# The state-scan output of a selective-scan and expert layer kept in bf16 instead of f32

## The chip, the cores and the metric

The kernel runs on the 8 cores of one Trainium2 chip, each with two of the 16 sequences of the batch and no exchange between them. The time is that of the device for the slowest core, in microseconds (us).

## The reference

What is computed, cut to the part that matters, is one layer: a normalised input goes through a selective scan (16 states per channel, 1024 channels, 2048 steps per sequence) and through a feed-forward part with a shared and eight routed experts, and the sum of both is added to the input.

```python
# selective scan (per sequence; D = 1024 channels, N = 16 states, G = 8 groups)
xp = xn @ in_proj_w.T + in_proj_b;  u, v = split(xp)
delta = softplus(u @ delta_proj_w.T);  A = -exp(a_log)
Bmat = (u @ b_proj_w.T + b_proj_b).reshape(B, L, G, N)
u_conv = silu(causal_conv(u, conv_w, conv_b))
dA = exp(delta[..., None] * A);  dBu = (delta * u_conv)[..., None] * Bexp
def step(h, xs):
    da, dbu = xs
    h = da * h + dbu
    y = einsum('bdn,dn->bd', h, c_param)
    return h, y
attn = y * silu(v)
# feed-forward: shared expert, plus top 2 of 8 routed experts on one hidden tensor
out = x + attn + swiglu(xn @ w_shared_in) @ w_shared_out \
        + sum_e wdense[:, e] * (swiglu(xn @ w1_shared) @ w2[e])
```

## The kernel before, in words

Each core treats its 2 x 2048 positions in 8 chunks of 512 (TC), four per sequence. A chunk has four stages, each a block with a barrier at its end: normalisation and transposition (L392 to L470), the projections (L472 to L555), the main stage (`emit_main`, from L632) and the output (L563 to L600). Weights run through a ring of 8 slots of 256 KB that SyncE (SP) fills from a bf16 copy in memory, 4 slots per transfer (`emit_pulls`, L322).

The main stage first does the short convolution for the 8 groups of 128 channels, on ScalarE and VectorE, while GpSimd forms du, the product of the convolution and delta (L834). Then it runs 128 steps j: group gg = j // 16, state n = j % 16. In a step

- TensorE (PE) broadcasts the row of B for this state, multiplied with c, to all channels, into pBCb (L949);
- ScalarE (ACT) computes dA = exp(A * delta) (L686);
- VectorE (DVE) multiplies du with pBCb into dBu (L819), in bf16, and then runs the recurrence over the 512 positions as one instruction, `tensor_tensor_scan`, from dA, dBu and the carried state into hsc (L824);
- GpSimd (POOL) copies the last column of hsc into the carried state stt_t (L849) and adds hsc to the group's sum ysc (L853; for n = 0 it copies, L851). After the sixteenth state it multiplies ysc with v_s, the gate, into acc (L858).

dA, dBu, hsc, ysc and pBCb each have two buffers. In the first chunk of each sequence the scan starts from 0.0 and not from the state, which is why its group shows in two forms (256 and 768 instructions).

The feed-forward work is placed between these steps by tables of numbers written by hand: T_GAPS for TensorE (gate and shared products L880 and L897, routed experts L932), A_EVS for ScalarE, P_INS for GpSimd (the products a_s * b_bf into smid and hid, L845), and V_INS for VectorE (the products hid * gate into hg, L786; the sum over experts into racc, L803 and L805; acc plus the shared result, L795). All engines run their instructions in the order in which they are written. VectorE waits for sp_y, GpSimd's counter of finished sums, of two steps before; GpSimd waits for sv_sc, the scan's counter; ScalarE waits for the scan that has read dA's buffer.

The lines that the change touches are L252, where hsc is allocated; L824, which writes it; and L849, L851 and L853, which read it.

Of the kernel before, what the change touches and what calls it, by code (L numbers as in the profile page):

```python
# [7 lines left out]
F32 = mybir.dt.float32  # L8
BF16 = mybir.dt.bfloat16
# [9 lines left out]
TC = 512  # L19
# [178 lines left out]
def build(dbg=False):  # L198
# [33 lines left out]
    with ExitStack() as ctx:  # L232
        en = ctx.enter_context

        def T(name, shape, dt):
            return en(nc.sbuf_tensor(name, shape, dt))

        env = {}
# [10 lines left out]
        b_sb = env["b_sb"] = T("b_sb", [32, 4, TC], BF16)  # L249
        dA = env["dA"] = T("dA", [128, 2, TC], F32)  # L250
        dBu = env["dBu"] = T("dBu", [128, 2, TC], BF16)
        hsc = env["hsc"] = T("hsc", [128, 2, TC], F32)  # L252
        stt_t = env["stt_t"] = T("state", [128, 128], F32)
        ccr = env["ccr"] = T("ccr", [128, 8, 3], BF16)
        ysc = env["ysc"] = T("ysc", [128, 2, TC], F32)
# [711 lines left out]
```

## Time and profile before

| what | us |
|---|---|
| median of 2 runs | 5287.13 (5264.27 to 5309.99) |
| the profiled execution, device time | 5258.23 |
| its span on the slowest core, from the first to the last instruction | 5256.7 |
| spans of all cores | 5234.7 to 5256.7 |
| busy: TensorE, VectorE, ScalarE, GpSimd | 2774.2, 3250.8, 1676.8, 1870.2 |

The profile is of the slowest core, core 5. Its times are read as follows: an engine's busy time is the sum over its instructions; a group of instructions is all those of one line, engine, operation and shape; idle time stands with the instruction in front of which it lies, and with what ended it. A duration is from the start of an instruction to its end, whatever it may wait for in between.

### The profile page before, as it was taken

Reading aid. Unit: us, or ns where it says so; the run is one execution under the profiler, and the core shown is the slowest. Engines: PE = TensorE matmul, PEld = TensorE weight load, DVE = VectorE, ACT = ScalarE, POOL = GpSimd, SP = SyncE. Lnnn points to the kernel's source line nnn. Section 1 sums busy time; section 2 is a strip of 40 time slices with the busy share of each in tenths; the row PEclk is TensorE's granted clock in tenths of the full one; section 3 lists DMA queues with packets and bytes.
Section 4 is the critical chain, followed back from the end, with each engine's and each line's share of the span. In section 5 each row is a group of like instructions: output and inputs, shape, how many; then the busy total and the mean of one; then the engine's idle time right before and its main releaser. Section 6 shows DMA issues by size and latency. Waiting matters only on the chain. (4 is left out here: it accounts for less than half of the span.)

```text
span 5256.7 us, 45388 instructions; the slowest of 8 cores (5234.7 to 5256.7 us)
## 1 busy us (share of the span) xinstructions
PE 2774.2 (53%) x10240; PEld 1030.3 (20%) x10240; DVE 3250.8 (62%) x4304; ACT 1676.8 (32%) x2403; POOL 1870.2 (36%) x2320
## 2 busy tenths in 40 slices
PE   0025763556625755357635566257563576355663
PEld 0012221212202222122212122022221222121221
DVE  0014788268863788447882688637884478826886
ACT  0014522353214712245213532147121452225321
POOL 0002544045430645126440454306441264403543
PEclk9997886678857988578866788568875788666885
DMA  9961121212211221112202122112211122121120
GB/s 104 110 94 66 66 83 42 82 40 75 83 35 64 74 74 67 42 64 72 85 34 82 42 74 86 46 50 74 74 67 40 59 74 82 42 80 43 67 90 19
DMA packets 51106, 348.50 MB, mean 66 GB/s; under 512 B 6368, under 2 KB 6624, under 8 KB 17024
## 3 DMA queue, kind: packets, MB, share of 16 engines
q1 hardware_dynamic: 46144, 302.30, 16.6%
q0 software_dynamic: 1632, 34.92, 6.2%
q10 hardware_dynamic: 3072, 8.39, 0.5%
q8 instruction: 95, 1.56, 0.1%
q14 instruction: 163, 1.34, 0.1%
HBM read 363.72 MB, written 51.38 MB: 79 GB/s over the span
## 5 line engine op out<-in xcount | busy, mean ns | idle before, releaser
L686 ACT ACTIVATE dA<-dlt,A_sb 128x512 f32<-128x512 bf16 x1024 | 740.1, 724 | 2009.5 <-DVE hsc L824 2007.4
L824 DVE TENSOR_TENSOR_SCAN hsc<-dA,state,dBu 128x512 f32<-128x512 f32 x768 | 1309.3, 1705 | 81.5 <-DVE dBu L819 1.8
L932 PE MATMUL pEG<-hg,ring 128*128 128x512 bf16 x4096 | 1013.6, 404 | 603.7 <-DVE hg L786 409.5
L853 POOL TENSOR_TENSOR ysc<-hsc,ysc 128x512 f32<-128x512 f32 x960 | 1234.0, 1285 | 2.0 <-issue 2.0
L819 DVE TENSOR_TENSOR dBu<-du,pBCb 128x512 bf16<-128x512 bf16 x1024 | 685.4, 669 | 458.4 <-PE pBCb L949 395.2
L849 POOL COPY state<-hsc 128x1 f32<-128x1 f32 x1024 | 242.3, 237 | 1661.4 <-DVE hsc L824 1645.1
L834 POOL TENSOR_TENSOR du<-du,dlt 128x512 bf16<-128x512 bf16 x64 | 73.6, 1150 | 1662.3 <-ACT du L673 1662.3
L932 PEld LDWEIGHTS pEG<-hg,ring 128*128 128x128 bf16 x4096 | 403.6, 103 | 1205.2 <-issue 831.9
L949 PE MATMUL pBCb<-b_sb,csel_sb 32*128 32x512 bf16 x1024 | 389.0, 422 | 418.6 <-DVE dBu L819 380.4
L824 DVE TENSOR_TENSOR_SCAN hsc<-dA,dBu 128x512 f32<-128x512 f32 x256 | 432.8, 1690 | 27.9 <-DVE dBu L819 1.8
L469 PE MATMUL pT<-ident,xnp 128*128 128x128 f32 x256 | 96.7, 446 | 583.6 <-DVE xnp L434 564.8
L880 PE MATMUL pAB<-xn_fm,ring 128*128 128x512 bf16 x1024 | 317.5, 466 | 78.7 <-ACT b_bf L700 78.6
L411 DVE TENSOR_SCALAR_CACHE_REDUCE uc<-x_tok 128x1024 f32<-128x1024 f32 x32 | 39.0, 1220 | 468.7 <-PEq L352 349.9
L590 PE MATMUL pT<-ident,accb 128*128 128x128 f32 x256 | 114.2, 446 | 306.6 <-DVE accb L574 306.6
L880 PE MATMUL pFF<-xn_fm,ring 128*128 128x512 bf16 x1024 | 249.7, 388 | 35.2 <-ACT b_bf L700 35.2
L728 DVE SCALAR_TENSOR_TENSOR uc<-u_pad,wcv_sb,uc 128x512 f32<-128x512 bf16 x192 | 165.1, 860 | 134.7 <-ACT uc L669 121.0
L949 PEld LDWEIGHTS pBCb<-b_sb,csel_sb 32*128 32x128 bf16 x1024 | 76.5, 94 | 747.6 <-issue 747.2
L720 DVE COPY u_pad<-ccr 128x24 bf16<-128x24 bf16 x6 | 1.1, 190 | 336.6 <-PEq L473 336.6
L786 DVE TENSOR_TENSOR hg<-hid,gb 128x512 bf16<-128x512 bf16 x512 | 207.9, 480 | 0.0
L579 DVE TENSOR_TENSOR x_tok<-x_tok,pT 128x128 f32<-128x128 f32 x256 | 73.8, 288 | 206.5 <-PE pT L590 206.5
L867 PE MATMUL pEG<-ident,lg 8*128 8x8 f32 x32 | 5.9, 220 | 352.5 <-DVE gt_tok L738 343.8
L686 ACT ACT_TABLE_LOAD x128 | 164.2, 1283 | 31.3 <-DVE hsc L824 28.3
(95 smaller groups left out, 2849.4 us busy)
## 6 DMA issues: line engine op xcount, KB each, us to landing
ring<-wsbf SPq DMA_DIRECT2D x256, 1024.0 KB, 4.8
wsbf<-wstream POOLq DMA_DIRECT2D x8, 4096.0 KB, 187.9
x_tok<-x SPq DMA_DIRECT2D x8, 2048.0 KB, 8.1
out<-x_tok SPq DMA_DIRECT2D x8, 2048.0 KB, 7.7
csel_sb<-cselbf ACTq DMA_DIRECT2D x64, 128.0 KB, 2.3
cselbf<-csel POOLq DMA_DIRECT2D x1, 1024.0 KB, 338.2
wbp_sb<-wbp POOLq DMA_DIRECT2D x1, 256.0 KB, 335.9
selc_sb<-selc SPq DMA_DIRECT2D x1, 128.0 KB
```

The source lines that it names most:

```text
L469: t.transpose(pT[:, j % 2, 0:128], xnp[:, j % 2, :], ident3[:]).then_inc(S.st_xp, 1)
L590: t.transpose(pT[:, j % 2, 0:128], accb[:, j % 2, :], ident3[:]).then_inc(S.st_op, 1)
L686: sc.activation(dA[:, j % 2, :], dlt[:, gg, :], AF.Exp, scale=A_sb[:, gg, n:n + 1]).then_inc(S.sa_da, 1)
L728: ins = v.scalar_tensor_tensor(uc[:, gg % 2, :], u_pad[:, gg, k:k + TC], wcv_sb[:, gg, k:k + 1], uc[:, gg % 2, :], ALU.mult, ALU.add)
L786: ins = v.tensor_tensor(hg[:, ii, kc, :], hid[:, kc, :], gb[:, e, :], ALU.mult)
L819: v.tensor_tensor(dBu[:, j % 2, :], du[:, gg, :], pBCb[:, j % 2, :], ALU.mult).then_inc(S.sv_bc, 1)
L824: v.tensor_tensor_scan(hsc[:, j % 2, :], dA[:, j % 2, :], dBu[:, j % 2, :], init, ALU.mult, ALU.add).then_inc(S.sv_sc, 1)
L849: gp.tensor_copy(stt_t[:, j:j + 1], hsc[:, j % 2, TC - 1:TC])
L853: ins = gp.tensor_tensor(ysc[:, gg % 2, :], hsc[:, j % 2, :], ysc[:, gg % 2, :], ALU.add)
L880: ins = t.matmul(pp[:, half, :], ring_piece(p_idx)[:, kc, :], xn_fm[:, kc, :], start=(kc == 0), stop=(kc == NK - 1))
L932: ins = t.matmul(pEG[:, m % 2, :], ring_piece(p_idx)[:, kc, :], hg[:, ii, kc, :], start=first, stop=(ii == 1 and kc == NK - 1))
L949: t.matmul(pBCb[:, j % 2, :], csel_sb[:, gg % 2, n, :], b_sb[:, s_, :], start=True, stop=True).then_inc(S.st_bc, 1)
```

## The change

The scan's output tile hsc is allocated in bf16 instead of f32. The scan instruction writes bf16, and GpSimd's three instructions that read hsc read bf16. The carried state, ysc, dA and dBu keep their types.

```diff
@@ -249,7 +249,7 @@
         b_sb = env["b_sb"] = T("b_sb", [32, 4, TC], BF16)
         dA = env["dA"] = T("dA", [128, 2, TC], F32)
         dBu = env["dBu"] = T("dBu", [128, 2, TC], BF16)
-        hsc = env["hsc"] = T("hsc", [128, 2, TC], F32)
+        hsc = env["hsc"] = T("hsc", [128, 2, TC], BF16)
         stt_t = env["stt_t"] = T("state", [128, 128], F32)
         ccr = env["ccr"] = T("ccr", [128, 8, 3], BF16)
         ysc = env["ysc"] = T("ysc", [128, 2, TC], F32)
```

No instruction changes its place. On GpSimd the copies out of hsc become conversions. This is GpSimd's order in the main stage at the end of a group of 16 states, before:

```order
L849 COPY state<-hsc 128x1
L853 TENSOR_TENSOR ysc<-hsc,ysc 128x512
L858 TENSOR_TENSOR acc<-ysc,v_s 128x512
L849 COPY state<-hsc 128x1
L851 COPY ysc<-hsc 128x512
```

And the same place in the changed kernel:

```order
L849 CAST state<-hsc 128x1
L853 TENSOR_TENSOR ysc<-hsc,ysc 128x512
L858 TENSOR_TENSOR acc<-ysc,v_s 128x512
L849 CAST state<-hsc 128x1
L851 CAST ysc<-hsc 128x512
```

The order is the same; L849 and L851 are CAST where they were COPY, and the additions of L853 have the same name with another type of input.

## Rows read from the trace of the kernel before

**Rows 1.** The page: span, and busy time of each engine.
```profile
span 5256.7 us, 45388 instructions; the slowest of 8 cores (5234.7 to 5256.7 us)
PE 2774.2 (53%) x10240; PEld 1030.3 (20%) x10240; DVE 3250.8 (62%) x4304; ACT 1676.8 (32%) x2403; POOL 1870.2 (36%) x2320
```

**Rows 2.** Busy time by stretch: the main stage of the second chunk, with its columns.
```profile
core 5: us, PE busy (x) PEld busy (x) DVE busy (x) ACT busy (x) POOL busy (x), PEclk, DMA share, GB/s
1103.00:1521.00 418.00, 265.42 (x970) 93.23 (x970) 343.99 (x355) 154.12 (x202) 221.77 (x279) 0.81 0.20 68
```

**Rows 3.** Groups by line: busy us, mean ns of one, idle before it and its releasers.
```profile
L824 DVE TENSOR_TENSOR_SCAN hsc<-dA,state,dBu 128x512 f32<-128x512 f32 x768 | 1309.3, 1705 | 81.5 <-DVE dBu L819 1.8
...
L819 DVE TENSOR_TENSOR dBu<-du,pBCb 128x512 bf16<-128x512 bf16 x1024 | 685.4, 669 | 458.4 <-PE pBCb L949 395.2 <-POOL ysc L853 45.8 <-POOL ysc L851 11.4
L824 DVE TENSOR_TENSOR_SCAN hsc<-dA,dBu 128x512 f32<-128x512 f32 x256 | 432.8, 1690 | 27.9 <-DVE dBu L819 1.8
```

**Rows 4.** Timeline of VectorE from 1254 us: start us, us, engine, line, instruction.
```profile
1254.04 1.28 DVE L824 TENSOR_TENSOR_SCAN hsc<-dA,state,dBu 128x512 f32<-128x512 f32 x1
1255.24 0.66 DVE L819 TENSOR_TENSOR dBu<-du,pBCb 128x512 bf16<-128x512 bf16 x1
1256.00 1.99 DVE L824 TENSOR_TENSOR_SCAN hsc<-dA,state,dBu 128x512 f32<-128x512 f32 x1
1257.92 0.66 DVE L803 COPY racc<-pEG 128x512 f32<-128x512 f32 x1
1258.50 0.67 DVE L819 TENSOR_TENSOR dBu<-du,pBCb 128x512 bf16<-128x512 bf16 x1
1259.28 1.40 DVE L824 TENSOR_TENSOR_SCAN hsc<-dA,state,dBu 128x512 f32<-128x512 f32 x1
```

**Rows 5.** Timeline of GpSimd beside it; in brackets its idle time before, and the releaser.
```profile
1255.51 0.18 POOL L849 COPY state<-hsc 128x1 f32<-128x1 f32 x1 [13.01 <-DVE hsc L824]
1255.65 1.26 POOL L853 TENSOR_TENSOR ysc<-hsc,ysc 128x512 f32<-128x512 f32 x1
1258.19 0.18 POOL L849 COPY state<-hsc 128x1 f32<-128x1 f32 x1 [1.28 <-DVE hsc L824]
1258.33 1.27 POOL L853 TENSOR_TENSOR ysc<-hsc,ysc 128x512 f32<-128x512 f32 x1
```

**Rows 6.** Timeline of GpSimd at the end of a group of 16 states.
```profile
1265.10 1.89 POOL L858 TENSOR_TENSOR acc<-ysc,v_s 128x512 f32<-128x512 f32 x1
1267.11 0.93 POOL L849 COPY state<-hsc 128x1 f32<-128x1 f32 x1
1267.98 0.61 POOL L851 COPY ysc<-hsc 128x512 f32<-128x512 f32 x1
```

**Rows 7.** Timeline of VectorE beside it, the two scans.
```profile
1264.63 1.40 DVE L824 TENSOR_TENSOR_SCAN hsc<-dA,state,dBu 128x512 f32<-128x512 f32 x1
...
1266.71 1.35 DVE L824 TENSOR_TENSOR_SCAN hsc<-dA,state,dBu 128x512 f32<-128x512 f32 x1
```

**Rows 8.** Single lines: ns min/median/max of one, first and last start us, forms.
```profile
L824 DVE TENSOR_TENSOR_SCAN hsc<-dA,dBu x256: 1224/1754/2311, 486.8 to 3351.5; 128x512 f32<-128x512 f32 x128
...
L853 POOL TENSOR_TENSOR ysc<-hsc,ysc x960: 1253/1264/2267, 490.4 to 5203.8; 128x512 f32<-128x512 f32 x192
...
L849 POOL COPY state<-hsc x1024: 174/183/1175, 488.3 to 5203.7; 128x1 f32<-128x1 f32 x171
...
L851 POOL COPY ysc<-hsc x64: 606/608/613, 488.4 to 5165.3; 128x512 f32<-128x512 f32 x64
...
L858 POOL TENSOR_TENSOR acc<-ysc,v_s x64: 1151/1890/2145, 538.4 to 5205.2; 128x512 f32<-128x512 f32 x64
...
L834 POOL TENSOR_TENSOR du<-du,dlt x64: 1145/1149/1153, 439.1 to 4769.4; 128x512 bf16<-128x512 bf16 x64
```

**Rows 9.** Who waited for L824's scan; what ended L819's idle time (us, times).
```profile
  POOL state L849: 1645.1, 811
...
  PE pBCb L949: 395.2, 198
```

## The prediction

> **What bounds the kernel now.** I read the engine totals first. VectorE (DVE) is the busiest engine with 62% of the span, and GpSimd (POOL) works 36% of it [rows 1]. No engine is near full, so the totals alone name no bound. The chain that ended last is of no use here: it goes back only through the output stage of the last chunk.
>
> Next, busy time by stretch. The main stage of the second chunk lasts 418 us, in which VectorE works 344 us and GpSimd 222 us [rows 2]. The change touches only instructions of this stage. Eight such stages are some 3.3 ms of 5.26 ms.
>
> Then the groups by line. The scans (L824) are the dearest: 1309.3 + 432.8 = 1742.1 us for 1024 of them, a mean of 1.70 us [rows 3]. Single scans differ widely, though all have one shape, and the timeline shows why. The scan at 1254.04 takes 1.28 us, and no GpSimd instruction runs beside it. The one at 1256.00 takes 1.99 us, and it starts while L853's add runs, which lasts from 1255.65 to 1256.91 [rows 4, 5]. The slow scan ends at 1257.99, 1.08 us behind the end of the add. The next one starts at 1259.28 and ends at 1260.68, again 1.08 us behind the end of an add (1258.33 + 1.27 = 1259.60). In the other direction L858 takes 1.89 us where its shortest takes 1.15 [rows 8]: it starts at 1265.10, the scan beside it ends at 1266.03, and it ends 0.96 us later, at 1266.99. The scan that started at 1266.71 ends 1.07 us behind that [rows 6, 7]. So a scan and a GpSimd instruction that reads SBUF don't run through together here: whoever came second ends as if it had begun to stream when the first was done.
>
> The Trainium skill, page "SBUF — State Buffer", section "Who interferes with whom", says the same: a VectorE instruction with two SBUF inputs contends with a GpSimd instruction that reads SBUF, and the loser blocks fully. By this rule the trace agrees (1.08 us behind the add, three times). Without it GpSimd would have slack and this change would be worth nothing.
>
> That gives the chain of one step. Scan j ends at 1255.32. GpSimd's 128x1 copy (L849) starts 0.19 us later, the add (L853) 0.14 us after that, takes 1.26 us, and scan j+1 ends 1.08 us behind it: 0.19 + 0.14 + 1.26 + 1.08 = 2.67 us, and scans do end at 1255.32, 1257.99 and 1260.68. By its semaphores VectorE waits little for GpSimd (45.8 + 11.4 us before L819 in the whole span) [rows 3], and it shows no idle time for this chain: the wait stands inside the scan's own duration. L853 is thus on the path, though its engine is idle for 1.27 us in each step.
>
> **The change part by part.** hsc, the scan's output, becomes bf16. Nothing is moved on any engine, and no wait is added or taken away. Four kinds of instruction touch hsc.
>
> 1. L853, 960 times, now reads bf16 (hsc) and f32 (ysc) and writes f32. Before, both inputs are f32 and it takes 1.253 us at least and 1.264 in the median. The trace has other two-input GpSimd instructions of the same 512 columns: L858 (f32 and bf16 in, f32 out) with 1.151 us at least, and L834 (all bf16) with 1.149 in the median [rows 8]. Both are multiplications while L853 is an addition, so the 0.11 us between them may belong to the type or to the operation; nothing in the trace tells these apart. The ends are 1.15 us (type) and 1.26 us (operation). Above them, should the addition convert its bf16 input in a pass of its own, at the rate of L851's copy (0.608 - 0.183 = 0.425 us for 511 columns), it would be 1.69 us. I take 1.151, the row with exactly the new mix of types: 1.264 - 1.151 = 0.113 us less.
>
> How often does this reach the end? 811 times GpSimd's L849 waited for the scan [rows 9], which are the steps in which the chain above starts afresh. 198 times VectorE sat idle before L819 until TensorE had delivered (395 us together) [rows 9]; there a scan that ends earlier only lengthens this idle time, if TensorE doesn't itself come earlier. I take all 198 off: 811 - 198 = 613 steps x 0.113 = 69 us. With all 811 it would be 92 us. In the steps with an expert accumulation (L803) between two scans, the scan is held up by only 1.40 - 1.28 = 0.12 us [rows 4], so the 0.113 still fits, but a second 0.1 us would find VectorE itself as the bound.
>
> 2. L849, 1024 times, becomes a conversion (CAST) of one column. From its start to that of the add it holds the chain for 0.14 us. L851's copy shows that columns cost 0.83 ns each, so the 0.18 us of L849 are fixed cost. It can't give back more than 0.14 us (613 x 0.14 = 86 us), and if its fixed cost doubled it would take as much. No GpSimd conversion stands in the trace. I take zero, the nearest row being the copy itself.
>
> 3. L851, 64 times, becomes a conversion of 512 columns: 0.61 us now. Between the fixed 0.18 us and a two-input instruction's 1.15 us this is -27 to +35 us. I take zero.
>
> 4. L824, 1024 times, writes bf16 and reads as before. Between L819, which writes bf16, and L803, which writes f32, there is nothing (0.66 us both) [rows 4], so I take zero. Its free duration is twice theirs for the same columns, which is the recurrence and not the write, so I exclude a gain. A loss as large as the spread between the shortest scan (1.224) [rows 8] and the usual free one (1.28) would be 0.06 x 1024 = 57 us.
>
> Sum: the profiled execution took 5258 us (span 5257). 5258 - 69 = 5189 us, 1.3% less. The median of the two runs of before is 5287, with the profiled time near the lower of them (5264); I predict for runs like the profiled one.
>
> **A rule that speaks against it.** L834, all bf16, takes 1.149 us; less the fixed 0.183 of L849 this is 0.966 us for 512 columns, or 1.89 ns each, where L853 has 2.11 ns. The Trainium skill, page "GPSIMD Engine Reference", section "2.1 Instruction dispatch", calls about 2.5 cycles per element a floor of every two-input body, whatever the types, since both operands come through one port; at its 1.2 GHz that is an estimate of 2.08 ns. By that rule L853 can't get faster, which is the outcome of the first rival below, 5258 us. L853 agrees with the rule; L834 and L858 are below its floor, so the trace shows that it isn't one for every type or every operation.
>
> **The rivals.**
> - The 0.11 us belong to addition against multiplication. Then L853 stays at 1.26 us and the time at 5258 us (up to 5287 by the median). For it: both fast rows are multiplications, and L858 with one bf16 input is no slower than L834 with two, so bytes as such don't count. Against: an addition and a multiplication would have to cost differently on the same data path, while two f32 operands are twice the bytes of two bf16. The same time comes out if the steps counted above hide the gain, by TensorE.
> - Slower: conversion costs GpSimd a pass of its own. With 1.69 us for L853 the chain grows by 0.425 us in 613 steps: +261 us, 5519 us. It decides over 2% from 105 / 613 = 0.17 us per step, and the one-column CAST could add to it. Against: L858 takes a bf16 input at 1.15 us. For: an in-place addition with a bf16 first input and the CAST stand nowhere in the trace.
> - More than forecast: the add falls to 1.15 in all 811 steps (-92 us) and the CAST gives a few hundredths too, 0.03 x 613 = 18 us: 5148 us, 2.1% less. For: shorter steps bring TensorE's inputs earlier too. Against: the expert steps have only 0.12 us to give.
> - The change does nothing to speeds, as the scan has no bf16 output path of its own and the type is dealt with elsewhere: the order of instructions shows L849 and L851 as CAST and the scan's output tile as bf16, so I give this nothing.
>
> **How the numbers follow.** Forecast (5189, own range 5166 to 5215): 0.58. No change (5240 to 5300): 0.26. More than forecast (5100 to 5165): 0.09. Slower by a pass or by the CAST (over 5300): 0.07. The range reaches from 5145 to 5300. The bound of 2% is 105 us, about what a measurement of this kernel can tell from no change; the forecast with its 69 us is inside it. Faster by over 2%: 0.09; within 2%: 0.84; slower by over 2%: 0.07.
>
> **What would show it right or wrong.** Right: L853's median is about 1.15, scans of the held-up kind go from 1.99 to 1.88 us and still end 1.08 us behind the add, the scans' sum falls from 1742 by some 80 us, the free scan stays at 1.28, and the main stage goes from 418 to about 409 us. Operation, not type: L853 stays at 1.26. Wrong from the start: L853 is faster, but scans stay at 1.99, which would mean that they aren't held by the add's end. If L849 starts the add later than 0.14 us behind it, the CAST is to blame. If all this is right and idle time before L819 grows by tens of us, TensorE took the gain.

## The result, and the profile after

The changed kernel takes 5174.0 us (median of 11 runs, 5167.3 to 5238.4), the kernel before 5268.7 us in the runs beside it. The ratio is 0.9813 with a 95% interval of 0.9785 to 0.9841: 1.9% faster. Medians and ranges here are of all executions; the ratios leave out those in which the cores of one die show a lower granted clock and take longer. The profiled execution took 5168.05 us, 90.2 us less than that of before.

Read the totals first. The page of the changed kernel, span and busy time of each engine:

```profile
span 5166.5 us, 45196 instructions; the slowest of 8 cores (5146.2 to 5166.5 us)
PE 2717.3 (53%) x10048; PEld 1022.9 (20%) x10240; DVE 3188.5 (62%) x4304; ACT 1671.4 (32%) x2403; POOL 1752.9 (34%) x2320
```

GpSimd lost 117 us of busy time and VectorE 62 us [rows 1], though no instruction of VectorE got less to do. (TensorE's count of matmuls is lower because some records are missing, so its busy time can't be compared.)

The groups by line of the changed kernel, which answer to [rows 3] (busy us, mean ns of one, idle before it and its releasers):

```profile
L824 DVE TENSOR_TENSOR_SCAN hsc<-dA,state,dBu 128x512 bf16<-128x512 f32 x768 | 1267.7, 1651 | 81.5 <-DVE dBu L819 1.8
L853 POOL TENSOR_TENSOR ysc<-hsc,ysc 128x512 f32<-128x512 bf16 x960 | 1128.3, 1175 | 2.0 <-issue 2.0
...
L819 DVE TENSOR_TENSOR dBu<-du,pBCb 128x512 bf16<-128x512 bf16 x1024 | 684.4, 668 | 430.0 <-PE pBCb L949 389.1 <-POOL ysc L853 31.2 <-POOL ysc L851 5.0
L824 DVE TENSOR_TENSOR_SCAN hsc<-dA,dBu 128x512 bf16<-128x512 f32 x256 | 418.4, 1634 | 27.9 <-DVE dBu L819 1.8
```

The scans fell from 1742.1 to 1686.1 us, which is 56.0 of VectorE's 62 us. The idle time before L819 fell by 28.4 us, from 458.4 to 430.0. Of these, 21.0 us are waits for GpSimd (45.8 + 11.4 before, 31.2 + 5.0 now) and 6.1 us are waits for TensorE (395.2 to 389.1). VectorE's shorter instructions and this shorter idle time are 62.3 + 28.4 = 90.7 us together, which is about the gain of the profiled execution, 90.2 us.

Single lines of the changed kernel, which answer to [rows 8] (ns min/median/max):

```profile
L824 DVE TENSOR_TENSOR_SCAN hsc<-dA,dBu x256: 1223/1884/2218, 486.2 to 3297.7; 128x512 bf16<-128x512 f32 x128
...
L853 POOL TENSOR_TENSOR ysc<-hsc,ysc x960: 1147/1158/2147, 489.7 to 5113.1; 128x512 f32<-128x512 bf16 x192
...
L849 POOL CAST state<-hsc x1024: 173/183/1192, 487.6 to 5113.0; 128x1 f32<-128x1 bf16 x171
...
L851 POOL CAST ysc<-hsc x64: 607/608/613, 487.7 to 5076.0; 128x512 f32<-128x512 bf16 x64
```

L853 went from 1.264 to 1.158 us. The two conversions cost what the copies cost: 183 and 608 ns in the median. The shortest scan, 1223 ns, is as short as before, so writing bf16 is worth nothing to the scan itself.

Timelines of VectorE and of GpSimd in the same place of the order as [rows 4] and [rows 5], in the changed kernel:

```profile
1237.09 1.28 DVE L824 TENSOR_TENSOR_SCAN hsc<-dA,state,dBu 128x512 bf16<-128x512 f32 x1
...
1239.05 1.89 DVE L824 TENSOR_TENSOR_SCAN hsc<-dA,state,dBu 128x512 bf16<-128x512 f32 x1
...
1242.22 1.29 DVE L824 TENSOR_TENSOR_SCAN hsc<-dA,state,dBu 128x512 bf16<-128x512 f32 x1
```

```profile
1238.56 0.18 POOL L849 CAST state<-hsc 128x1 f32<-128x1 bf16 x1 [13.44 <-DVE hsc L824]
1238.70 1.16 POOL L853 TENSOR_TENSOR ysc<-hsc,ysc 128x512 f32<-128x512 bf16 x1
1241.14 0.18 POOL L849 CAST state<-hsc 128x1 f32<-128x1 bf16 x1 [1.28 <-DVE hsc L824]
```

The add ends at 1239.86 and the scan at 1240.94, 1.08 us behind it, as before. The held-up scan went from 1.99 to 1.89 us with the add, and the one that follows L803 from 1.40 to 1.29. In the last one nothing is left: 1.28 us is a scan that nobody holds up.

### The profile page after: what moved, and what is told of

It reads as the page before. It is cut to its first block and busy times, and to the rows that moved or that the text cites. A ratio compares the mean times of both kernels' runs of the same rounds, so it can differ in the third digit from the quotient of the medians.

```text
span 5166.5 us, 45196 instructions; the slowest of 8 cores (5146.2 to 5166.5 us)
## 1 busy us (share of the span) xinstructions
PE 2717.3 (53%) x10048; PEld 1022.9 (20%) x10240; DVE 3188.5 (62%) x4304; ACT 1671.4 (32%) x2403; POOL 1752.9 (34%) x2320
## 5 line engine op out<-in xcount | busy, mean ns | idle before, releaser
L824 DVE TENSOR_TENSOR_SCAN hsc<-dA,state,dBu 128x512 bf16<-128x512 f32 x768 | 1267.7, 1651 | 81.5 <-DVE dBu L819 1.8
L932 PE MATMUL pEG<-hg,ring 128*128 128x512 bf16 x4000 | 999.7, 404 | 579.6 <-DVE hg L786 392.7
L853 POOL TENSOR_TENSOR ysc<-hsc,ysc 128x512 f32<-128x512 bf16 x960 | 1128.3, 1175 | 2.0 <-issue 2.0
L819 DVE TENSOR_TENSOR dBu<-du,pBCb 128x512 bf16<-128x512 bf16 x1024 | 684.4, 668 | 430.0 <-PE pBCb L949 389.1
L849 POOL CAST state<-hsc 128x1 f32<-128x1 bf16 x1024 | 227.8, 222 | 1687.3 <-DVE hsc L824 1673.4
L949 PE MATMUL pBCb<-b_sb,csel_sb 32*128 32x512 bf16 x1024 | 386.6, 420 | 404.7 <-DVE dBu L819 362.6
L824 DVE TENSOR_TENSOR_SCAN hsc<-dA,dBu 128x512 bf16<-128x512 f32 x256 | 418.4, 1634 | 27.9 <-DVE dBu L819 1.8
L880 PE MATMUL pAB<-xn_fm,ring 128*128 128x512 bf16 x992 | 298.7, 451 | 81.3 <-ACT b_bf L700 76.2
L786 DVE TENSOR_TENSOR hg<-hid,gb 128x512 bf16<-128x512 bf16 x512 | 204.5, 472 | 0.0
L469 PEld LDWEIGHTS pT<-ident,xnp 128*128 128x128 f32 x256 | 46.5, 182 | 633.3 <-issue 624.7
```

Of the source, the lines that this page charges most:

```text
L469: t.transpose(pT[:, j % 2, 0:128], xnp[:, j % 2, :], ident3[:]).then_inc(S.st_xp, 1)
L786: ins = v.tensor_tensor(hg[:, ii, kc, :], hid[:, kc, :], gb[:, e, :], ALU.mult)
L819: v.tensor_tensor(dBu[:, j % 2, :], du[:, gg, :], pBCb[:, j % 2, :], ALU.mult).then_inc(S.sv_bc, 1)
L824: v.tensor_tensor_scan(hsc[:, j % 2, :], dA[:, j % 2, :], dBu[:, j % 2, :], init, ALU.mult, ALU.add).then_inc(S.sv_sc, 1)
L849: gp.tensor_copy(stt_t[:, j:j + 1], hsc[:, j % 2, TC - 1:TC])
L853: ins = gp.tensor_tensor(ysc[:, gg % 2, :], hsc[:, j % 2, :], ysc[:, gg % 2, :], ALU.add)
```

## The experiments

Theory "lock": a scan that meets a GpSimd instruction which reads SBUF ends 1.08 us behind it, so that GpSimd's duration is on the path although its engine is idle for most of the time. Theory "type": L853 got shorter because one of its inputs is bf16. Rivals: additions differ from multiplications; the gain came with the scan's output or from GpSimd's load as such. All ratios are to the kernel before, run on the same chip.

**L853 as a multiplication, all in f32.** Kernel before, and the sum over states is left out:

```diff
-                                       ysc[:, gg % 2, :], ALU.add)
+                                       ysc[:, gg % 2, :], ALU.mult)
```

> Kernel before (hsc in f32), with L853 multiplying instead of adding; the sum over states is left out. Theory 'type' (two f32 inputs cost more than a pair with a bf16 one): L853 stays at 1.26 us and the time at that of before, about 5269 us, within 0.3%. Rival 'operation' (multiplications are faster on GpSimd than additions): L853 falls to 1.15 us and the time to about 5174 us, as the change gives.

Measured: 5261.7 us, ratio 1.0012 (0.9984 to 1.0040). L853 of this run:

```profile
L853 POOL TENSOR_TENSOR ysc<-hsc,ysc x960: 1252/1265/2258, 493.2 to 5221.3; 128x512 f32<-128x512 f32 x192
```

The median is 1265 ns against 1264 for the addition. "Operation" is out: the 0.11 us belong to the types. The time fell as expected too, within 0.3% of that of before.

**The sum in bf16 as well.** Changed kernel, with ysc in bf16:

```diff
-        ysc = env["ysc"] = T("ysc", [128, 2, TC], F32)
+        ysc = env["ysc"] = T("ysc", [128, 2, TC], BF16)
```

> Changed kernel, with the running sum ysc in bf16 too, so that L853 reads and writes bf16 alone. Theory 'floor' (one bf16 input already reaches what L834 has with two): L853 stays at 1.15 us and the time at that of the changed kernel, 5174 us, within 0.3%. Rival 'bytes' (each halved input takes 0.11 us off): L853 takes 1.05 us, and 811 steps x 0.11 = 89 us are gained again, 5085 us.

Measured: 5196.4 us in the median (5154.3 to 5227.2), ratio 0.9854 (0.9781 to 0.9928). The median is 0.4% above 5174, a little more than the 0.3% allowed, but the interval holds the changed kernel's 0.9813. L853:

```profile
L853 POOL TENSOR_TENSOR ysc<-hsc,ysc x960: 1139/1150/2149, 494.2 to 5164.4; 128x512 bf16<-128x512 bf16 x192
```

The second bf16 input, together with a bf16 output, is worth 8 ns (1158 to 1150) where the first was worth 106. "Bytes" is out, and "floor" holds for the duration. The time alone, with its interval of 0.7% to each side, would have told less than the line does; 5085 us would have been a ratio of about 0.965 and lies outside it.

**Only the sum in bf16.** The same line changed in the kernel before, so that hsc, the scan and L849 stay in f32.

> Kernel before with hsc left in f32 and only the running sum ysc in bf16. The scan, L849 and the input hsc are those of before. Theory 'lock and type' (the gain comes from L853's own duration alone, and it is any bf16 input that shortens it): L853 takes 1.15 us, held-up scans go from 1.99 to 1.88 us, and the time is that of the changed kernel, 5174 us, within 0.5%. Rival 'scan' (the gain comes with the scan's bf16 output, or with hsc as the first input): 5269 us, as before.

Measured: 5182.7 us, ratio 0.9851 (0.9807 to 0.9894), against 0.9813 (0.9785 to 0.9841) of the change itself. Groups by line:

```profile
L824 DVE TENSOR_TENSOR_SCAN hsc<-dA,state,dBu 128x512 f32<-128x512 f32 x768 | 1273.0, 1658 | 81.3 <-DVE dBu L819 1.8
L853 POOL TENSOR_TENSOR ysc<-hsc,ysc 128x512 bf16<-128x512 f32 x960 | 1122.0, 1169 | 2.0 <-issue 2.0
```

A scan that still writes f32 fell from 1309.3 to 1273.0 us in sum [rows 3], about as with the change (1267.7). So the scan's output type is not what shortened the scans; the add's duration is. (In this run the add's output is bf16 as well as its second input.)

**Half the add.** Changed kernel; the other 256 columns of the sum are left out:

```diff
-                ins = gp.tensor_tensor(ysc[:, gg % 2, :], hsc[:, j % 2, :],
-                                       ysc[:, gg % 2, :], ALU.add)
+                ins = gp.tensor_tensor(ysc[:, gg % 2, 0:256], hsc[:, j % 2, 0:256],
+                                       ysc[:, gg % 2, 0:256], ALU.add)
```

> Changed kernel, with L853 adding only the first 256 of 512 columns; the rest of the sum is left out. L853 should take 0.18 + 256 x 1.89 ns = 0.67 us, 0.49 us less. Theory 'lock': in a step without an expert accumulation a scan is held up until the add has ended, so the step goes from 2.57 to 2.08 us; in the 256 steps with one (L803, L805) the scan is hardly held up already and nothing is gained. (811 - 256) x 0.49 = 272 us, 4900 us, and up to 5000 us where TensorE or ScalarE becomes late. Rival 'GpSimd has slack' (its duration isn't on the path, the gain came otherwise): 5174 us, as the changed kernel.

Measured: 4985.8 us in the median of four (4910.1 to 5063.2), ratio 0.9336 (0.9291 to 0.9381). The two shortest executions, which the ratio is of, took 4910.1 and 4914.5 us, where 4900 had been expected. Single lines, of L824 and L853:

```profile
L824 DVE TENSOR_TENSOR_SCAN hsc<-dA,state,dBu x768: 1283/1319/2233, 1050.3 to 4859.0; 128x512 bf16<-128x512 f32 x192
...
L853 POOL TENSOR_TENSOR ysc<-hsc,ysc x960: 661/671/1586, 484.8 to 4860.7; 128x256 f32<-128x256 bf16 x192
```

The add takes 0.671 us, as worked out (0.67), and the median scan went from 1.88 to 1.32. VectorE's and TensorE's work is unchanged, and the kernel is 4.9% faster than the changed one (0.9336 / 0.9813). That is a gain of some 250 us from GpSimd alone, near the 272 expected; "GpSimd has slack" is out. A scan and the add that it meets, from the timelines of this run:

```profile
1188.42 1.40 DVE L824 TENSOR_TENSOR_SCAN hsc<-dA,state,dBu 128x512 bf16<-128x512 f32 x1
```

```profile
1188.07 0.67 POOL L853 TENSOR_TENSOR ysc<-hsc,ysc 128x256 f32<-128x256 bf16 x1
```

The add ends at 1188.74 and the scan at 1189.82, again 1.08 us later: the distance stays the same when the add is half as long.

**The scan reads one input from PSUM.** Kernel before. PSUM is the memory that TensorE writes its results to, and pBCb lies in it. L819 writes its product over pBCb, the scan takes it from there, and TensorE waits for the scan before it overwrites the buffer:

```diff
-            v.tensor_tensor(dBu[:, j % 2, :], du[:, gg, :],
+            v.tensor_tensor(pBCb[:, j % 2, :], du[:, gg, :],
                             pBCb[:, j % 2, :], ALU.mult).then_inc(S.sv_bc, 1)
...
-                                 dBu[:, j % 2, :], init,
+                                 pBCb[:, j % 2, :], init,
...
-                t.wait_ge(S.sv_bc, C_SVBC * c + j - 1)
+                t.wait_ge(S.sv_sc, C_SVSC * c + j - 1)
```

> Kernel before (hsc in f32), with L819 writing its product in place into pBCb in PSUM, and the scan reading it from there, so that the scan has only one input in SBUF. TensorE may overwrite a buffer of pBCb only after the scan, no longer after L819. Theory 'lock' (only a VectorE instruction with two SBUF inputs is held up): every scan takes about 1.28 us whatever GpSimd does, their sum falls from 1742 to about 1310 us, and up to 430 us are gained: 4840 us if nothing else is late, 5000 us where TensorE or ScalarE is. Rival 'no lock' (scans are held up in another way, as by the memory as such): scans stay at 1.99 us in the median and the time at 5269 us, or above it because TensorE waits longer.

Measured: 4852.3 us (4847.9 to 4858.8), ratio 0.9224 (0.9201 to 0.9247). (The 1.99 us in the expectation are the held-up scan of [rows 4]; the median of all scans before was 1.75 to 1.81.) All 1024 scans, and L849:

```profile
L824 DVE TENSOR_TENSOR_SCAN hsc<-dA,state,pBCb x768: 1279/1280/1283, 1056.4 to 4802.8; 128x512 f32<-128x512 f32 x192
L824 DVE TENSOR_TENSOR_SCAN hsc<-dA,pBCb x256: 1219/1221/1222, 490.6 to 3108.5; 128x512 f32<-128x512 f32 x128
...
L849 POOL COPY state<-hsc x1024: 176/183/191, 492.0 to 4804.2; 128x1 f32<-128x1 f32 x171
```

No scan is held up any more: the spread from shortest to longest is 4 ns, where it was over 1000. GpSimd isn't held up by scans either; its one-column copy took up to 1175 ns [rows 8] and takes 191 at most. The timeline shows both running through each other, VectorE first, then GpSimd:

```profile
1190.30 0.67 DVE L819 TENSOR_TENSOR pBCb<-du,pBCb 128x512 f32<-128x512 bf16 x1
1191.08 1.28 DVE L824 TENSOR_TENSOR_SCAN hsc<-dA,state,pBCb 128x512 f32<-128x512 f32 x1
```

```profile
1190.71 1.26 POOL L853 TENSOR_TENSOR ysc<-hsc,ysc 128x512 f32<-128x512 f32 x1
```

The add runs from 1190.71 to 1191.97, the scan begins inside it at 1191.08 and yet takes 1.28 us. This is the sharpest test of the lock. The same run holds a control: L786, a VectorE product whose two inputs still lie in SBUF, goes on being held up. 32 of its 512 instructions take 1.48 to 1.50 us where the median is 0.415, and each of them ends 0.28 us behind the end of the add that it meets.

```profile
L786 DVE TENSOR_TENSOR hg<-hid,gb x512: 398/415/1497, 614.0 to 4719.6; 128x512 bf16<-128x512 bf16 x171
```

What the run shows is that the hold-up needs both inputs in SBUF. That it is a port which the two engines share, and not another part of the memory, is not shown by it. This version also beats both kernels of the study, with hsc in f32.

**The same with hsc in bf16.** The change under study, on top of the version above.

> As e5_psum_f32, but with hsc in bf16: the change under study on top of a scan that reads one input from PSUM. Theory 'lock' (the change pays only through the add that holds up the scan): L853 takes 1.15 instead of 1.26 us, but the time is that of e5_psum_f32 within 0.3%. Rival 'any other way' (the scan's output or GpSimd's own load pays): some 90 us less than e5_psum_f32, as between the two kernels of the study.

Measured: 4842.9 us, ratio 0.9205 (0.9181 to 0.9228). Groups by line, of this run:

```profile
L853 POOL TENSOR_TENSOR ysc<-hsc,ysc 128x512 f32<-128x512 bf16 x960 | 1118.6, 1165 | 2.0 <-issue 2.0
L824 DVE TENSOR_TENSOR_SCAN hsc<-dA,state,pBCb 128x512 bf16<-128x512 f32 x768 | 982.8, 1280 | 81.3 <-DVE pBCb L819 1.8
```

L853 is 0.1 us shorter here too and GpSimd saves 101 us of busy time (1690.1 to 1588.9), but the kernel gains only some 10 us, 0.2% and within the 0.3% expected, where the same edit was worth 95 us. The 768 scans of this row take 982.8 us in both versions, whatever they write. So nearly all of the change's value goes by the scan that the add holds up. What little is left shows in a row of its own. These two are what L819 waited for, in the version with f32 and in this one (us, times):

```profile
  POOL ysc L853: 20.5, 11
...
  POOL ysc L853: 8.3, 5
```

VectorE waits openly for GpSimd's sums in a few steps, and these waits fell by 12.2 us. That second way is open in the two kernels of the study too (45.8 to 31.2 us before L819).

**The state column behind the add.** Changed kernel; L849's copy is moved:

```diff
-            gp.tensor_copy(stt_t[:, j:j + 1], hsc[:, j % 2, TC - 1:TC])
             if n == 0:
...
-            ins.then_inc(S.sp_y, 1)
+            gp.tensor_copy(stt_t[:, j:j + 1], hsc[:, j % 2, TC - 1:TC]
+                           ).then_inc(S.sp_y, 1)
```

> Changed kernel, with L849's state column behind L853 instead of ahead of it. The add then starts 0.14 us earlier behind the scan. Theory 'lock': held-up scans go from 1.88 to 1.75 us; in the 256 steps with an expert accumulation there is nothing left to gain, so (811 - 256) x 0.14 = 78 us, 5096 us. Rival 'the column gets in the way' (L849 now comes second behind the scan, waits for its end with 0.9 us and delays the next add): no gain or a loss, 5174 to 5250 us.

Measured: 5136.3 us (5108.1 to 5175.6), ratio 0.9749 (0.9683 to 0.9815); the profiled execution took 5109.5 us, against 5168.1 of the changed kernel. Timelines of GpSimd and, below it, of VectorE (L852 is the add here, L854 the state column):

```profile
1216.78 1.17 POOL L852 TENSOR_TENSOR ysc<-hsc,ysc 128x512 f32<-128x512 bf16 x1 [0.23 <-DVE hsc L824]
1217.88 1.11 POOL L854 CAST state<-hsc 128x1 f32<-128x1 bf16 x1
1219.23 1.16 POOL L852 TENSOR_TENSOR ysc<-hsc,ysc 128x512 f32<-128x512 bf16 x1 [0.23 <-DVE hsc L824]
```

```profile
1214.99 1.57 DVE L824 TENSOR_TENSOR_SCAN hsc<-dA,state,dBu 128x512 bf16<-128x512 f32 x1
1216.65 0.69 DVE L819 TENSOR_TENSOR dBu<-du,pBCb 128x512 bf16<-128x512 bf16 x1
1217.44 1.58 DVE L824 TENSOR_TENSOR_SCAN hsc<-dA,state,dBu 128x512 bf16<-128x512 f32 x1
```

The mechanism is as expected: the scan ends at 1219.02, 1.07 us behind the add's end at 1217.95, and scans follow each other in 2.46 us instead of 2.57. The column now waits out the scan (1.11 us for one column) and is done with it. The size is less than expected: 5096 us is a ratio of about 0.967, outside the interval. The interval alone also leaves it nearly open whether anything was gained, since the changed kernel's 0.9813 is just inside. The traces settle that: from the end of its first scan to the end of its last, the eight main stages together are 51 to 70 us shorter than in the changed kernel, on each of the eight cores, 60 us in the mean. The 78 us of the expectation used a wrong step. The add starts 0.22 us behind the scan (1216.78 - 1216.56) where it was 0.33, so that moving the column saves 0.11 us and not 0.14, and (811 - 256) x 0.11 = 61 us. In the rows L819 also starts 0.09 us behind the scan's end, where it started 0.08 before it. The likely reason is that sp_y is now counted by L854, which ends with the scan, at 1218.99; VectorE waits openly for it in 45 steps, 41.0 us together.

## Why the prediction was right

The predicted time was 5189 us in a range of 5145 to 5300; measured were 5174. The change of 1.9% lies within the 2% that held most of the chance, though its interval, 1.6% to 2.15%, reaches just past. Part of the closeness is luck: the forecast took 69 us off 5258, and measured were 95 us off 5269, so that a start 11 us higher hides some of the 26 us by which the gain was underrated.

- **The chain of one step** was right. The scan still ends 1.08 us behind the add, and all seven experiments fit it: half the add gives some 250 us more, and a scan with one input in PSUM makes the hold-up go away altogether. (Of the three ends that the prediction counts as 1.08 us behind the add, two are; the third is 1.07 us behind the multiplication of L858.)
- **The rule of the Trainium skill on the shared port** (page "SBUF — State Buffer", section "Who interferes with whom"), by which the trace agreed, is now borne out by a run and not by three ends alone: same work, one input moved to PSUM, and the scans' hold-ups are gone in both directions.
- **L853 falls to 1.151 us** was nearly right: 1.158. The choice between type and operation, which nothing in the trace of before could settle, was settled by the multiplication in f32 (1.265).
- **The rule that speaks against it**, about 2.5 cycles for every two-input body (the Trainium skill, page "GPSIMD Engine Reference", section "2.1 Instruction dispatch"), fits two f32 inputs (1.264 and 1.265 us) and not a pair with a bf16 one (1.158, 1.152, 1.150 us). The section itself says nothing of types; "whatever the types" is the prediction's reading.
- **CAST at nothing, L851 at nothing, the scan's write at nothing**: 183, 608 and 1223 ns, all as before.
- **The count of steps** was mis-sized. The sum was 613 steps x 0.113 = 69 us; the profiled executions differ by 90.2 us. At 1.264 - 1.158 = 0.106 us that would be 851 steps, more than the 811 of the upper bound. The step that failed is the count "811 - 198 = 613". It is made of waits of GpSimd and of VectorE, where held-up scans should have been counted. In the trace of before, 817 of the 1024 scans take over 50 ns longer than a free one. VectorE had waited for TensorE in front of 57 of these, and in front of 760 it had not. So of the 198 steps taken off, 141 had no held-up scan to lose; and the 811 leave out the steps in which GpSimd came late and L849 found the scan done, behind which another 147 scans were held up. 760 x 0.106 = 81 us. The other 9 us were not assigned to steps; open waits are among them, since VectorE's idle time before L819 that GpSimd ended is 21.0 us less.

  The two kernels side by side, from the end of one scan to the end of the next, agree with that. On each of the eight cores 685 to 699 steps are 0.085 to 0.125 us shorter, 72 to 73 us together, of the 87 us by which the main stages fell in the mean of the cores. At the 152 places where VectorE waits for TensorE in nearly every core of both kernels, the steps got no shorter, as the prediction had it (4 us longer together). But nothing that was won ahead of them was lost there: idle time in front of L819 that TensorE ended is 389.1 us and was 395.2 (384.6 and 385.6 in the mean of the cores). TensorE came earlier by as much as VectorE did, since it waits for VectorE in turn. Its row in the changed kernel:

```profile
L949 PE MATMUL pBCb<-b_sb,csel_sb 32*128 32x512 bf16 x1024 | 386.6, 420 | 404.7 <-DVE dBu L819 362.6 <-DMA csel_sb<-cselbf 41.3
```

  The 362.6 us that it waited for L819 had been 380.4.
- **The signs named beforehand.** The scans' sum fell by 56 and not by some 80 us: a part of the gain is in idle time. The main stage was to fall from 418 to about 409 us, and fell by a little more. From the first scan of the first chunk to the last of the fifth, with five main stages, it was 3351.5 - 486.8 = 2864.7 us [rows 8] and is 3297.7 - 486.2 = 2811.5, so 10.6 us each.
- **The rivals.** "Addition against multiplication" fell to the first experiment. "A pass of its own for the conversion" never came: every mixed or all-bf16 form took 1.15 to 1.16 us. "More than forecast" was half right: more steps counted than 613, but the CAST gave nothing.

## What to carry to other kernels

When instructions of one shape have very different durations on VectorE, lay the timeline of GpSimd beside them before you believe that GpSimd has slack: a hold-up inside an instruction counts as busy time and shows in no list of waits. The remedy here was to give the VectorE instruction only one input in SBUF (7.8% for three edited lines); with that done, shortening what GpSimd does was worth 0.2%. To find how often such a saving reaches the end, count the instructions that are themselves held up (817 here), and not another engine's waits (811) less a third one's (198): the three numbers overlap.

## What the runs showed of the hardware that was not expected

A scan whose start value is a column of SBUF takes 1280 ns, and one that starts from the constant 0.0 takes 1221 ns, for the same 512 columns; with no hold-ups in the way these are exact to 4 ns. The spread from 1.224 to 1.28 us that the prediction took as a bound for a write in bf16 was this.

On GpSimd the first bf16 input takes 106 ns off an add of 512 columns, and it hardly matters which of the two it is (1158 with hsc in bf16; 1152 with ysc, where the output is bf16 too). The second takes off 2 ns (1152 to 1150, with the same output).
